# Pairing the value blocks of the last two attention steps as in the first six

## The reference

```python
qkv = einsum('bsd,ed->bse', x, w_qkv) + b_qkv
scores = einsum('bhqd,bhkd->bhqk', q, k) / sqrt(32)      # causal mask
out = einsum('bhqk,bhkd->bhqd', softmax(scores), v)
h1 = layernorm(x + einsum('bsd,ed->bse', out, w_out) + b_out)
hidden = relu(einsum('bsd,hd->bsh', h1, sign(up_weight)) * up_scale)
y = einsum('bsh,dh->bsd', hidden, sign(down_weight)) * down_scale * output_scale
result = layernorm(h1 + y)
```

## Time and profile before

| | us |
|---|---|
| median of 3 runs | 782.07 |
| lowest and highest | 779.53, 782.5 |
| profiled execution | 783.35 |
| its span | 781.6 |
| TensorE busy | 730.8 |
| VectorE busy | 450.3 |
| GpSimd busy | 354.9 |
| ScalarE busy | 317.0 |

### The profile page before, as it was taken

How to read it: one execution, slowest core, us unless ns; L and a number is a source line. 1 busy time by engine, 2 the same in 40 slices (tenths; PEclk the granted TensorE clock), 3 DMA queues, 4 the chain that set the end, 5 groups by cost and what they waited for, 6 DMA issues and landing times.

```text
span 781.6 us, 11689 instructions
## 1 busy us (share of the span) xinstructions
PE 730.8 (94%) x4032; PEld 508.9 (65%) x4032; DVE 450.3 (58%) x1086; ACT 317.0 (41%) x631; POOL 354.9 (45%) x487
## 2 busy tenths in 40 slices
PE   6899999999999999999978989999999999999993
PEld 4688665655656556565534543788778787878882
DVE  4176496785957859578566651632295429434515
ACT  5211355554655546565446556423222222221210
POOL 4461467394674947648322501542344235323333
PEclk9999999999999999999989899999999999999997
DMA  6965454435545354442577240403003101000101
GB/s 228 297 188 146 127 178 133 137 109 149 161 135 145 91 161 139 129 143 83 152 225 243 83 136 27 149 28 122 14 28 107 24 5 41 15 1 0 55 1 54
DMA packets 44619, 85.71 MB, mean 110 GB/s; under 512 B 4880, under 2 KB 13584, under 8 KB 44432
## 3 DMA queue, kind: packets, MB, share of 16 engines
q1 hardware_dynamic: 35536, 79.72, 33.8%
q10 hardware_dynamic: 9024, 5.24, 2.4%
HBM read 55.33 MB, written 29.36 MB: 108 GB/s over the span
## 4 chain that ended last, share of the span: by engine, by line
PE 70%; DVE 20%; issue 3%; DMA 3%; ACT 2%; POOL 1%; SPq 0%; ACTq 0%; DVEq 0%; POOLq 0%
PE ps_heads L1043 9%; PE ps_proj L1085 7%; DVE heads_sb L833 7%; PE ps_proj L945 6%; PE ps_score L1102 6%; PE ps_unit L1061 6%; DVE maxes L811 6%; PE ps_sum L1037 6%; PE ps_unit L1085 5%; PE ps_unit L981 4%; PE ps_heads L1102 3%; PE ps_sum L1102 3%; PE ps_unit L1013 3%; DVE heads_sb L835 2%; PE ps_score L981 2%
## 5 line engine op out<-in xcount | busy, mean ns | idle before, releaser
L653 POOL TENSOR_TENSOR hid_low<-hid_raw,hid_high 128x512 fp32r<-128x512 f32 x64 | 85.0, 1329 | 175.2 <-DVE hid_high L884 172.1
L709 ACT ACTIVATE probs<-ps_unit 128x512 f32<-128x512 f32 (+3 forms) x215 | 101.1, 491 | 91.7 <-PE ps_unit L1013 87.9
L617 POOL TENSOR_SCALAR_AFFINE_SELECT probs<-probs 128x128 f32<-128x128 f32 x256 | 73.3, 296 | 129.6 <-ACT probs L709 125.1
L709 ACT ACTIVATE probs<-ps_score 128x512 f32<-128x512 f32 (+3 forms) x156 | 75.1, 496 | 76.2 <-PE ps_score L1013 73.8
L807 DVE CUSTOM_DVE_ANT_0 ps_unit<-ps_unit,causal 128x256 f32<-128x256 f32 (+3 forms) x164 | 80.4, 509 | 41.2 <-PE ps_unit L981 40.3
L884 DVE CAST hid_high<-hid_raw 128x512 fp32r<-128x512 f32 x64 | 27.1, 424 | 127.2 <-ACT hid_raw L764 126.9
L981 PE MATMUL ps_unit<-stack 96*128 96x512 f32 (+3 forms) x247 | 86.0, 363 | 7.6 <-DVE maxes L807 3.8
L1043 PE MATMUL ps_heads<-probs,v_rows 128*32 128x512 f32 (+3 forms) x768 | 81.9, 504 | 10.1 <-DVE heads_sb L835 10.1
L1013 PE MATMUL ps_unit<-stack 98*128 98x512 f32 (+2 forms) x215 | 77.8, 368 | 3.9 <-DVE maxes L807 3.9
L611 POOL TENSOR_TENSOR parts<-qk_full,parts 128x512 fp32r<-128x512 f32 x32 | 41.1, 1284 | 58.2 <-ACT parts L688 58.0
L981 PEld LDWEIGHTS ps_unit<-stack 96*128 96x128 f32 x247 | 46.7, 193 | 31.6 <-DVE maxes L811 10.9
(11 more groups left out here) (195 smaller groups left out, 1456.7 us busy)
## 6 DMA issues: line engine op xcount, KB each, us to landing
stack<-qk_parts SPq DMA_DIRECT2D x96, 256.0 KB, 4.5
qk_parts<-parts SPq DMA_DIRECT2D x32, 512.0 KB, 2.8
v_all<-h_even ACTq DMA_DIRECT2D x16, 256.0 KB, 3.3
v_rows<-v_all SPq DMA_DIRECT2D x8, 512.0 KB, 4.6
heads_t<-heads_sb SPq DMA_DIRECT2D x16, 256.0 KB, 3.1
raw<-up_w SPq DMA_DIRECT2D x8, 512.0 KB, 3.5
x_tile<-x_rows SPq DMA_DIRECT2D x16, 256.0 KB, 5.0
raw<-down_w SPq DMA_DIRECT2D x8, 512.0 KB, 3.9
```

What stands on the lines that cost most here:

```text
L653: nc.gpsimd.tensor_tensor(hid[1][:, (HM * s + n) % 3, :], hid_raw[:, n % 2, :], hid[0][:, (HM * s + n) % 3, :].bitcast(FP32), ALU.subtract ...
L709: nc.scalar.activation(probs[:, (NP * s + n) % RING, 0:width], bank(what, s, n)[:, off:off + width], ACT.Exp, scale=SCALE).then_inc(s_exp, 1)
```

## The change

The two tables of single places for the last steps, one for each, are gone. Step 6 takes `PAIRED` and `PAIRED_NORM` of the first six steps. Step 7 takes the same but for the last pair (blocks 10 and 11), which stands at slot 49 with its normalizations at 49.05, between `up` 0 (48.5) and `up` 1 (49.5); before, block 10 was at 46, and block 11 at 48.6 between the same two. The late projections of step 6 take the places of the first six steps: block 2 from slot 0.5 at 0.98 a matmul (before 4.2 at 0.48), block 3 from 13.3 at 0.5 (before 11.9 at 0.45); evictions go from slot 9.9 to 13.05 and from 17.1 to 19.65, stores from 12.5 to 15.8 and 19.9 to 22.4, fills from 14.9 to 18.5 and 22.2 to 24.8. `shift` 7.1, the jobs, `attn`, `y` and the turns keep their slots.

```diff
-ALONE = [[11.2, 13.5, 15.7, 18.3, 24, 28, 31.5, 36, 39.5, 43, 46.5, 50.3],
-         [10, 12.4, 15, 17.5, 24, 28, 31.5, 35, 38.5, 42.5, 46, 48.6]]
-ALONE_NORM = [[18.4, 18.41, 18.42, 18.43, 50.4, 50.41, 50.42, 50.43],
-              [17.6, 17.61, 17.62, 17.63, 48.7, 48.71, 48.72, 48.73]]
+LAST_PAIRED = PAIRED[:10] + [49, 49]
+LAST_NORM = PAIRED_NORM[:4] + [49.05, 49.06, 49.07, 49.08]
...
-LAST_BLOCK = [(1, 2, 4.2, 0.48, 9.9, 12.5, 14.9), (1, 3, 11.9, 0.45, 17.1, 19.9, 22.2)]
+LAST_BLOCK = BLOCK[:2]
...
-        paired = s < STEPS - 2
-        for g, at in enumerate(PAIRED if paired else ALONE[s % 2]):
+        last_step = s == STEPS - 1
+        for g, at in enumerate(LAST_PAIRED if last_step else PAIRED):
...
-        for q, at in enumerate(PAIRED_NORM if paired else ALONE_NORM[s % 2]):
+        for q, at in enumerate(LAST_NORM if last_step else PAIRED_NORM):
```

## The result

| | before | after |
|---|---|---|
| median, us | 779.52 (6 runs) | 787.52 (6 runs) |
| lowest and highest | 777.48, 782.5 | 785.64, 789.35 |
| profiled execution | 783.35 | 788.63 |
| its span | 781.6 | 786.9 |

The changed kernel takes 1.0097 times the time of the kernel before (95% interval 1.008 to 1.0115): slower by 1%, 8 us on the medians. The forecast was 784.4, with a change too small to measure as the likeliest case (0.60). The range of 778 to 789 holds 787.52, but the sum of +2.3 us was far too small. Further down, a gain or loss in us is the difference of two ratios times 780 us, unless it is said to be of medians or of a trace.

A forecast was written before the change was run, and what follows sets the result against it. TensorE, busy 94% of the span, was taken as the bound, so its work or idling counts. First up 1.3 us late plus 1.0 for block 10 gave +2.3 on 782.07: 784.4 us, range 778 to 789.

The forecast's parts named there:

- the template: Step 5's TensorE timeline, set 48.4 us later, as the pattern for paired step 6; 7.8 us from pair 4,5 to 6,7.
- the fall of the clock at pair 8,9: Step 6, second half: half clock makes the pair take 5.2 us instead of 3.3, costing 1.9 us.
- attention output 24: Step 7, first half: it waits for VectorE's first residual behind four normalizations, leaving TensorE 1.1 us idle.
- Rival B: Step 6, second half: the clock holds over pair 8,9, 1.9 us less, 782.5 us; chance 0.20.
- rival C: Step 6, first half: fill landed when normalizations end, pair 4,5 ends 4.8 us earlier, 779.6 us; chance 0.15.
- The fill's landing: Step 6, first half: block 2's fill, issued at 395.0 behind two weight loads, lands and releases maximum 16 at 402.0.
- upper bound: Latest landing of block 2's fill: 2.5 us for 1 MB of weights, then 4.9 us, 402.4.
- Rival D: Ahead of step 7's attention output: the clock falls before the turn, costing 3.4 us, 787.8 us; chance 0.20.
- A: The sum over steps 6 and 7 as forecast: +2.3 us, 784.4 us, own range 781 to 787; chance 0.45.
- The row maximum: End of step 6: 3.5 us from the end of pair 8,9 to the turn of the row maxima at 436.7.
- Step 7's second half: From block 3 to the first up: 32.3 us, including 2.8 for half clock over the pair; up at 490.7, 1.3 behind.
- the end: Behind step 7's first up: blocks 10 and 11 both stand there, before only 11, costing 1.0 us more.

The follow-up runs named there:

- e12: Kernel before with only step 6's late projections moved to the first six steps' places, value blocks single: 786.08 us, 1.0084 of before.
- e1: Changed kernel with SyncE's two output-weight jobs at slot 18.6 instead of 17.2, so the fill of block 2 goes first: 784.22 us, 1.0052 of before.
- e5: Changed kernel with GpSimd's four output-bias additions moved ahead to slot 44.1 of step 6: 785.78 us, 1.0068 of before.
- e11: Changed kernel with both the weight-load jobs behind the fill of block 2 and GpSimd's bias additions at 44.1: 781.1 us, 1.0023 of before.
- e2: Changed kernel with step 7 back in its old single places, step 6 still paired: 783.38 us, 1.0027 of before.
- e4: Changed kernel with the weight-load jobs behind the fill and step 7 in its old single places: 780.39 us, 1.0006 of before.
- e10: Changed kernel with 22 extra matmuls, results unread, ahead of step 7's first turn of h1 only: 786.89 us, 1.0082 of before.
- e3: Kernel before with only step 7 paired, step 6 and late projections as before: 784.28 us, 1.0051 of before.
- e6: Changed kernel with extra matmuls, results unread, in TensorE's waits of steps 6 and 7: 784.17 us, 1.005 of before.
- e7: Kernel of e4 with extra matmuls, results unread, at eight places in waits of steps 6 and 7: 776.78 us, 0.996 of before.
- e8: Kernel before with 34 extra matmuls, results unread, at six places in steps 6 and 7: 776.14 us, 0.9946 of before.
- e9: Kernel of e8 with GpSimd's bias additions moved early, to slots 44.1 to 44.4 of step 6: 777.33 us, 0.996 of before.

## Why the prediction was right or wrong

**What held.** Step by step, each time counted from the first mark:

| us behind the first mark | forecast | after |
|---|---|---|
| fill issued, behind both weight loads | 17.3 | 16.8 |
| TensorE idle until | 24.3 | 26.2 |
| end of pair 4,5 | 32.1 | 34.1 |
| start of pair 6,7 | 39.9 | 41.9 |
| start of pair 8,9 | 50.3 | 52.6 |
| its end | 55.5 | 57.6 |
| turn for step 7 | 59.0 | 62.0 |

The queue order on SyncE, the wait that it makes, the half clock over pair 4,5, the paces (8.0 us from the wait to the pair's end, 7.8 forecast; 7.7 from there to pair 6,7, 7.8 forecast by the template), the fall of the clock at pair 8,9 and its price (5.0 us for the pair, 5.2 forecast) all came. In step 7: attention output 24 idle for 0.90 us (1.1), block 3 to the first turn 9.06 (9.05), 6.01 us idle there (6), the pair 11.4 us behind block 3 (11.3), block 3 to `up` 32.6 (32.3). Rival B fell with the clock at 0.50 in 430:432, rival C with the fill that ended the wait.

**What failed, in order of size.**

1. *The fill's landing, +1.9 us.* The step "1 MB at 0.41 MB/us, then 4.9 us" gave 7.0 us from issue to release (402.0); it took 9.3 (393.17 to 402.51), less 0.5 because the issue came earlier. Two things are in it. The fill is three transfers, and maximum 16 needs all of them. They landed 6.8, 7.5 and 8.4 us after their own issues, in before 3.5, 4.5 and 5.2. So the 7.4 us of the upper bound fits the middle one, but the sum counted it from the first issue, while the third is issued 0.9 us later and lands last. The upper bound (402.4) was thus no upper bound. And the second leg isn't a plain 4.9: about 1 MB had moved by 396.0, as the sum has it, but then the DMA engines were busy for 0.85 and 0.89 of the time at 125 and 70 GB/s. SyncE had issued the store of block 3, another 0.5 MB, at 395.70; the prediction has it behind the fill but at no price. How much of the second leg is the store's wasn't measured. In e12, with the same order of issues, the three landed after 6.9, 7.6 and 8.3 us. e1 prices the whole place at 3.5 us.

2. *Rival D came on top of A, +1.6 us.* I gave it 0.20 as a case of its own, deciding by when the turn comes. The clock fell at 439.5, and from the turn to the end of block 3 it took 23.3 us instead of 21.7. It took 21.7 and 21.8 in e5 and e11, where the clock didn't fall, so the 1.6 us are the fall's; D had 3.4 for a fall twice as long. (The terms that the prediction names for this stretch add up to 22.2, not to the 21.7 that it uses: a slip of 0.5 that came out right.) The forecast let the lateness of the turn decide. The runs with step 6 paired sort by how long TensorE stood in front of it: 2.01 us in after and 2.00 in e1, e2, e4 and e10, each with a fall 0.9 to 1.6 us behind the turn; 0.92 in e5 and 0.93 in e11, without one.

3. *The row maximum, +1.0 us.* The 3.5 us from pair to turn were taken from the earlier trace rows, step 5, where GpSimd adds no bias. It took 4.45. The additions kept their slots while VectorE's work moved against them; the prediction went through SyncE's queue for such neighbours but not GpSimd's. This term cost 1.0 us itself and brought on point 2, since e5's fall is gone with it: e5 gave 2.3 us back by the ratios.

4. *Step 7's second half, +0.3, and the end, -0.6.* Both small. The 2.8 us that the sum added for the clock over pair 4,5 is above what e10 bears out (0.7 to 2.4). If it was too much, another term of the 32.3 was too short by as much; which one wasn't measured. These terms, with 0.1 to 0.2 us for rounding and small shifts, make the 4.3 us by which the two traces' difference of 6.6 passes the forecast's 2.3.

5. *The reference.* The forecast took the profiled execution as 1.3 us above the median of 782.07; over six runs the median of before is 779.52, so it was 3.8 above. With 779.52 the same sum gives 781.9, and the range, moved along, is 775.5 to 786.5, which doesn't hold 787.52. That the range held is luck: the first three executions of the kernel before have a median 2.5 us above that of all six, and this made up for 2.5 of the 5.7 us by which the change was underrated.

The costs by the runs: fill 3.5 us, GpSimd's addition with the fall behind it 2.3, step 7's pairs the rest, 1.8 by e11, and 4.0 and 5.5 where they are added to or taken from kernels that have other falls of the clock (e3, and e2 against after). These last do not add up with the others, since each edit also moves the falls. Each is uncertain by some 2 us, as the intervals are 0.2% wide to either side. The template for pairs gains some 2 us in step 6 in e11's trace, and step 7 takes it back. The kernel with all three mended (fill first, additions early, step 7 single) wasn't run; e4's 1.0006 less 0.29% gives 0.998 as an estimate. In step 7 the pair stands behind a turn of h1 that VectorE makes late, and a single block 4 had filled 1.85 us of that wait.

## What to carry to other kernels

When a block of work takes over the slots of another stage, read every queue that it now passes, and beside it what the other engines have at those slots and the template's stage hadn't: here SyncE's weight loads and GpSimd's additions made three quarters of the loss (0.74 of 0.97%). Count a wait for several transfers from the issue of the last of them, and price what is issued beside them too. In this kernel a wait of two microseconds in front of dense matmuls was to be costed twice, once as a wait and once as half clock over what follows, at 0.2 to 0.3 us for each microsecond of half clock where other engines also bound the pace; and where waits can't be removed, matmuls that nobody reads, put into them, made this kernel 0.5% faster than any placement of its real work that was tried.

## What the runs showed of the hardware

- A row maximum of 128x16 on VectorE takes 0.17 us, and 1.23 to 1.29 us when it starts 0.02 to 0.06 us behind an addition of two SBUF tensors on GpSimd (after, e1, e2, e4, e6, e7, e8, e10); started 0.03 us ahead of it, 0.17 (before, e3, e12). A split of 128x512 takes 0.69 us alone and 1.60 and 1.67 beside the additions (e9, e5). A shift of 0.07 us between two engines decides over 1.1.
- The clock fell to 1.2 GHz not only in standstills of 3.88 us (before, 401.2) and 6.26 (after, 398.6), but also in the second of two waits of 0.93 and 0.92 us (e1, 397.6) and 0.9 us behind one of 1.24 (after, 425.9). The Trainium skill has both kinds in "TensorE: Matmul & The Clock Gate": the long gap in "Why this matters for your kernels", and frequent micro-idles in "A second HAM failure mode: psum-queue depth-cycling". The second, which the prediction didn't weigh, is told there of a bf16 kernel whose PSUM banks are cycled; these rows agree that short waits are enough.
- Extra matmuls in the waits are worth 0.47% on after (e6), 0.46% on e4 (e7) and 0.54% on before (e8), though they add 61, 36 and 34 matmuls to the engine that is busy for 93% of the span. They took away 20.5, 13.7 and 13.7 us of half clock and saved 4.1, 3.9 and 3.4 us in the traces.
- Three 256 KB fills landed 3.5, 4.5 and 5.2 us after their issues in before, and 6.8, 7.5 and 8.4 us when issued right behind two weight loads of 512 KB and ahead of a store of 512 KB (after; e12 had 6.9, 7.6 and 8.3).
